# Moving the second token tile's load behind two key-weight loads, and its layer statistics behind the first value quarter

## The reference

```python
xn = _layernorm(x, axis=-1)
# attention, 16 heads of 32
Q = elu(xn @ wq.T + bq) + 1;  K = elu(xn @ wk.T + bk) + 1;  V = xn @ wv.T + bv
KV = einsum('bhsd,bhse->bhde', K, V)
out = einsum('bhsd,bhde->bhse', Q, KV) / (einsum('bhsd,bhd->bhs', Q, sum_s K)[..., None] + 1e-08)
attn = out @ wo.T + bo
# feed-forward, 1376 wide; router picks 2 of 8 experts of rank 8
gate = xn @ W_gate + lora + expert_lora;  up = xn @ W_up + lora + expert_lora
ffn = (silu(gate) * up) @ W_down + lora + expert_lora
return x + attn + ffn
```

## Time and profile before

| | |
|---|---|
| median of three runs | 669.9 us (669.51 to 671.44) |
| the profiled execution | 671.42 us, its span 669.6 us |
| PE busy | 659.4 us (98%) |
| DVE busy | 375.8 us (56%) |
| ACT busy | 257.5 us (38%) |
| POOL busy | 127.1 us (19%) |
| DMA, mean over the span | 74.21 MB, 111 GB/s |
| mean granted clock of PE | 0.997 of full |

### The profile page before, as it was taken

The page is one execution under the profiler, slowest core; times in us unless marked ns, Lnnn a source line. Parts: engine busy times, 40 slices in busy tenths (PEclk is TensorE's granted clock), DMA queues, the critical chain, the costliest instruction groups (busy, mean ns, idle before and its releaser), DMA issues.

```text
span 669.6 us, 10326 instructions
## 1 busy us (share of the span) xinstructions
PE 659.4 (98%) x3568; PEld 545.9 (82%) x3568; DVE 375.8 (56%) x698; ACT 257.5 (38%) x413; POOL 127.1 (19%) x290
## 2 busy tenths in 40 slices
PE   6999999999999999999999999999999999999998
PEld 5998999977777788888888888888888888888886
DVE  5677888778775956334345443445444326534433
ACT  4444454467235423323233333243233324323321
POOL 3466566626246230000000000000000000000000
PEclk8999999999999999999999999999999999999999
DMA  7875666644754679940025100011400001300001
GB/s 222 300 258 192 209 224 220 231 181 141 288 218 158 238 217 3 45 160 0 1 78 200 52 0 0 0 67 76 187 0 0 0 5 73 126 0 0 0 0 63
DMA packets 41642, 74.21 MB, mean 111 GB/s; under 512 B 19392, under 2 KB 20288, under 8 KB 39952
## 3 DMA queue, kind: packets, MB, share of 16 engines
q1 hardware_dynamic: 38672, 64.52, 34.6%
q10 hardware_dynamic: 2736, 9.05, 3.5%
q0 software_dynamic: 208, 0.30, 0.2%
HBM read 52.81 MB, written 21.04 MB: 110 GB/s over the span
## 4 chain that ended last, share of the span: by engine, by line
PE 94%; DVE 3%; DMA 1%; ACT 1%; issue 0%; SPq 0%; DVEq 0%
PE bank L1245 21%; PE bank L1246 21%; PE bank L1247 21%; PE bank L1490 18%; PE bank L1463 6%; DVE den L1091 2%; PE bank L1474 1%; PE bank L1476 1%; PE bank L1264 1%; DMA xin<-in_x 1%; PE bank L1276 1%; PE bank L1363 1%; PE bank L1501 1%; PE bank L1503 1%; PE bank L1285 0%
## 5 line engine op out<-in xcount | busy, mean ns | idle before, releaser
L1245 PE MATMUL bank<-x,up_h 128*128 128x512 f32 (+1 forms) x352 | 137.1, 390 | 0.2 <-DVE x3r L1056 0.2
L1247 PE MATMUL bank<-x,up_l 128*128 128x512 f32 (+1 forms) x352 | 137.0, 389 | 0.0
L1246 PE MATMUL bank<-x,up_h 128*128 128x512 f32 (+1 forms) x352 | 137.0, 389 | 0.0
L1182 DVE TENSOR_TENSOR hf<-bank,silu 128x512 f32<-128x512 f32 x44 | 30.4, 691 | 155.0 <-issue 135.3
L1490 PE MATMUL bank<-dn,hid_h 128*128 128x512 f32 x352 | 108.7, 390 | 0.0
L677 ACT ACTIVATE hid_h<-hf 128x512 fp32r<-128x512 f32 x44 | 27.8, 632 | 144.0 <-DVE hf L1182 144.0
L1245 PEld LDWEIGHTS bank<-x,up_h 128*128 128x128 f32 x352 | 66.1, 188 | 14.5 <-issue 0.7
L1490 PEld LDWEIGHTS bank<-dn,hid_h 128*128 128x128 f32 x352 | 65.9, 188 | 14.4 <-DVE res L1207 0.6
L1247 PEld LDWEIGHTS bank<-x,up_l 128*128 128x128 f32 x352 | 66.1, 188 | 13.8
L1246 PEld LDWEIGHTS bank<-x,up_h 128*128 128x128 f32 x352 | 66.1, 188 | 13.7
L888 DVE TENSOR_TENSOR up_l<-up_raw,up_h 128x1024 fp32r<-128x1024 f32 x44 | 54.9, 1249 | 28.1 <-ACT up_h L677 28.1
(11 more groups left out here) (166 smaller groups left out, 1083.4 us busy)
## 6 DMA issues: line engine op xcount, KB each, us to landing
x<-scr_x SPq DMA_DIRECT2D x7, 2048.0 KB, 8.5
up_raw<-in_ffn_up SPq DMA_DIRECT2D x11, 768.0 KB, 7.6
scr_x<-xt ACTq DMA_DIRECT2D x16, 512.0 KB, 4.5
xin<-in_x SPq DMA_DIRECT2D x16, 256.0 KB, 4.3
scr_z<-zt SPq DMA_DIRECT2D x16, 256.0 KB, 2.2
x3r<-in_x SPq DMA_DIRECT2D x16, 256.0 KB, 3.4
scr_att<-x3r SPq DMA_DIRECT2D x16, 256.0 KB, 2.8
z<-scr_z SPq DMA_DIRECT2D x4, 1024.0 KB, 4.8
```

Source lines behind the costliest of these rows:

```text
L1182: nc.vector.tensor_tensor(hf[:], ps_u[:], silu[:], ALU.mult).then_inc(h_done, 1)
L1245: nc.tensor.matmul(dst, lh, rh, start=start, stop=False, **kw)
L1246: nc.tensor.matmul(dst, lh, rl, start=False, stop=False, **kw)
L1247: return nc.tensor.matmul(dst, ll, rh, start=False, stop=stop, **kw)
```

## The change

SP starts the load of x tile 1 behind its two key quarters and ahead of the value quarters. DVE takes the statistics of that tile behind the low part of value quarter 0, where it had taken them ahead of all weights. No instruction is added or taken away.

```diff
@@ SyncE
             load_x(0, 0)
             sp.dma_start(ident[:], dram["ident"]).then_inc(ident_in, 16)
-            load_x(1, 1)
             for k in range(1, KD, 2):
                 sp.dma_start(w_raw[:, 0, k], dram["wkT"][:, k]).then_inc(wk_in[k], 16)
+            load_x(1, 1)
             for k in range(KD):
                 sp.dma_start(w_raw[:, 1, k], dram["wvT"][:, k]).then_inc(wv_in[k], 16)
@@ VectorE
             stats_of(0, 0, 0)
             normalise(0, 0)
-            stats_of(1, 1, 0)
 
...
             for k in range(KD):
                 dve.wait_ge(wseth_done, KD + k + 1)
                 sub(wv_l[:, k], w_raw[:, 1, k], wv_h[:, k]).then_inc(wsetl_done, 1)
+                if k == 0:
+                    stats_of(1, 1, 0)
                 if k == KD - 1:
                     normalise(1, 1)
```

## The result

The changed kernel takes **672.65 us** (median of nine, 670.88 to 674.54), the kernel before 669.67 us (median of nine, 669.23 to 671.44) in the same comparison. By the medians it is slower by 3.0 us or 0.44%, by the means by 2.7 us; the ratio is 1.004 with a 95% interval of 1.0024 to 1.0056. So it is slower beyond noise, while the interval's lower end, 0.24%, is under the 0.3% that the prediction took as the line. The profiled execution of the changed kernel took 673.9 us, its span 672.1 us, against 671.42 and 669.6.

What follows compares the result with a forecast made beforehand. PE was taken to bound the kernel, working without a pause that matters from its first product. The profiled 671.42 us plus 1.00 for the later key product of tile 1 gave 672.4 us, range 670.4 to 674.2.

Steps and rivals of the forecast that it cites:

- The deciding term: GpSimd's key-bias copy, queued behind rstd of tile 1, issues 4.03 us later; PE's key product of tile 1 starts 1.00 later.
- PE starts 0.38 earlier, and this does not come off: At the start, PE's first product comes at 9.89 instead of 10.27, but the 0.38 us won doesn't reduce the later loss.
- Value quarters cost nothing: On DVE, value quarters 1 to 3 delayed by the statistics cost PE nothing, with about 1 us to spare.
- Worth nothing by itself: SyncE's key quarters, issued 0.42 us earlier ahead of tile 1's load, bring no time by themselves.
- The base: Whole execution: 1.00 us is added to the profiled 671.42, not the median 669.9, since an early clock can't help the changed kernel.
- Rival (3): Whole execution: the 1.0 us shift is right but counts from the median 669.9, giving 670.9; chance 0.16.
- The step behind it: PE's first products: the 1.7 us gap between execution groups is a half-clock stretch, the lower pair having full clock.
- rival (1): PE's new idle time before tile 1's keys: the clock falls, another 3.4 us at half costs 1.7, giving 674.1; chance 0.22.
- Rival (2): Key-bias copy on GpSimd: lands by 17.0, 2.7 us after issue, so not slower, 671.0 or 669.3; chance 0.06.
- Rival (4): Start of DVE's work: key quarter 0 lands 0.4 us or more later, statistics at 12.55, giving 672.8; chance 0.06.

Runs made afterwards that it cites:

- e1: Changed kernel with GpSimd's key-bias copy moved ahead of rstd of tile 1; 669.28 us, ratio to the kernel before 0.9991.
- e6: Changed kernel with three more small GpSimd operations, results unused, between rstd of tile 1 and the key-bias copy; 675.80 us.
- e5: Kernel before with GpSimd's key-bias copy moved ahead of rstd of tile 1; 669.69 us, ratio 1.0012.
- e3: Kernel before with only the statistics of tile 1 moved, behind value quarter 0, the load left in place; 673.41 us.
- e2: Kernel before with only the load of tile 1 moved behind SyncE's key quarters, the statistics left in front; 672.59 us.
- e9: Kernel before, unchanged, run again for a second trace; one execution, 668.87 us.
- e10: Changed kernel, unchanged, run again for a second trace; one execution, 673.57 us.
- e8: Kernel before with ten instead of four products on the identity matrix ahead of the first key product; 669.91 us.
- e7: Changed kernel with the key-bias copy issued by SyncE instead of GpSimd, still waiting for rstd of tile 1; 671.81 us.
- e4: Changed kernel with six unused products on the identity matrix on PE behind the last products of tile 0; 672.37 us.

## Why the prediction was right

**The deciding term** was the bias copy behind rstd of tile 1. Forecast and first trace: statistics 12.16 and 11.64; issue 14.29 and 14.10; 4.2 and 4.2 us in flight; kb 18.52 and 18.34; seam 19.86 and 19.68. e1 shows it as the cause, e6 its slope, e5 that it needs the late statistics. Two small misses cancelled in part: key quarter 0 landed 0.56 earlier than I had left it, and rstd took 0.89 us instead of 0.56.

**"PE starts 0.38 earlier, and this does not come off."** It started 0.90 earlier (9.37), again through the key quarter; none of it arrived at the seam. Right.

**"Value quarters cost nothing."** Right for the end: PE waited 0.2 us for one, ahead of the hole. e1 has the same order without a loss.

**"Worth nothing by itself", of the load.** Right beside the moved statistics, as far as can be told (e3 and the changed kernel, 673.41 and 672.65 us, with overlapping executions). With the statistics left in front it costs 3 us (e2), since DVE then waits for the tile.

**The base.** This was the choice that mattered for the number. The sum gives 1.00 us at the seam against the first trace, and I left 672.4 against a median of 669.9, on the ground that an early full clock helps the old kernel and can't help the new one. e9 and e10 bear it out: 16.26 and 19.56. Rival (3), 670.9, falls. The step behind it is only partly right: the clock is not all of the 2.6 us between the two traces of before, since PE's first product also comes 1.45 us earlier in e9 (8.82 to 10.27), with the key quarter. I read the executions near 671.4 as those with the half clock; of the 13 executions of before at 670.6 us or more beside e1 to e8 (all up to 673), four show 0.997, one 0.999, the others 1.0. Those at 1.0 must have lost their time in a way that the mean clock doesn't show. The landing of the first key quarter, 7.92 and 6.19 us in two traces of one kernel, could do it, or a late rise of the clock at the start (last section), but no trace of such an execution exists here.

**The clock in the hole**, rival (1), got 0.22, and it came in five of nine executions. The failed step is the hole's length: I took half the clock in the first products, so a hole of 1.5 us, where the common case is a full clock and a hole of 2.5. The price (1.7) was right. So the median, 672.65, lies between the executions without a fall (about 672.3, where the forecast of 672.4 was) and those with one (mostly 673.0 to 674.5, where this rival was, 674.1). That the middle of the two groups is so near to 672.4 is luck; that each group is near its number is not.

**Rival (2)**, the bias in time, rested on a faster copy. It took 4.2 us again, also where the engines were nearly empty (a DMA share of 0.18 from 13.8 to 16.6 in e10), and 3.6 at best (e7). The small copies behind it took 4.7 to 4.9 us in the changed kernel instead of 3.2 to 3.5, and were still in time: `bq_c` issued at 15.98 landed near 20.8 and was read at 22.49.

**Rival (4)**, a late key quarter 0 (672.8), is near the measured median but did not occur: in the two traces of the changed kernel ACT had that quarter at 7.4 and 6.9, earlier than the 7.92 of the forecast, and the statistics started at 11.64 and 11.56.

## What to carry to other kernels

When an instruction is moved on one engine, look at what stands behind its consumer on the consumer's engine: here a tiny statistic fed GpSimd's rstd, behind which an unrelated copy with 4 us of latency was queued, and the copy became the path. Start such a copy before any wait that it doesn't need, and a reordering elsewhere can't reach it. And before adding a shift to a median, look at which early delays of the old kernel the new one would swallow: take a second trace if the executions fall into groups.

## What the runs showed of the hardware

The clock of PE did not always fall with the same hole. With 2.3 us (before, first trace), 2.5 us (changed, both traces), 2.0 us (e7), 2.9 us (e2) and 4.8 us (e6) of idle time it fell to half for 3.4 us; with 2.7 us (e3) it stayed full in the traced execution. The fall came at 19.3 in e10, before PE took up work at 19.56, and at 20.8 in the changed kernel's first trace, 1.1 us after PE took it up at 19.68. With all but 1.2 us of the hole filled none of seven executions shows 0.997 (e4).

The granted clock does not tell all at the start of the span. It reads 1.00 from 8.7 to 9.6 in e1, where a product took 0.63 us, as did those in the half-clock stretch of the first trace of before; from 10.25 on it took 0.40:

```profile
9.26 0.63 PE L1247 MATMUL bank<-wk_l,xt 128*128 128x512 f32 x1
```

The eight records on the identity matrix ahead of it took 1.91 us, and 1.14 us in the first trace of before. So the clock seems to come up at different times, and the mean clock of an execution doesn't include this.

The same small GpSimd operation (vare) took 0.19 us where DVE was idle at its start and 0.54 to 0.65 where DVE was inside an instruction (before, changed, e1 and e9, first 14 tiles). Rstd of tile 1 took 0.56 us in the earlier trace rows and 0.89 in the changed kernel, which lengthened the chain by 0.3.

The same 256 KB copy issued by GpSimd took 4.2 to 4.4 us where it was issued at 10.2 us or later (seven traces), and 4.5 (e5), 5.0 (e9), 5.2 (e8) and 5.5 us (e1) where it was issued at 9.8, 9.2, 9.4 and 8.4. These four and the one issued at 10.26 all landed between 13.9 and 14.6, about when the DMA share falls from 0.99 to 0.54; that they waited for the weights to be through fits this but was not tested. Issued early the copy takes longer and is in time all the same.
